# A fused attention block on one core: transposes of the first step in another order over more banks, and the decay of the queries behind the joins in every step

## What is computed

```python
xn = layernorm(x)                                   # 4 x 512 x 512
q, k, v = split(silu(xn @ w_qkv.T))                 # 16 heads of 128
for each chunk of each head:                        # kernel: chunks of 128 tokens
    o  = (q * q_decay) @ kv                         # what earlier chunks left
    o += ((q @ k.T) * diag_decay) @ v               # inside the chunk
    kv = block_decay * kv + (k * k_decay).T @ v
o = norm_w * o * rsqrt(mean(o * o) + eps)
s = (sigmoid(xn @ w_gate.T) * o) @ w_out.T
g = silu(xn * sum(topk(softmax(xn @ router.T))) + topk weights @ expert_bias)
out = x + s * g
```

## Time and profile before

| | us |
|---|---|
| median of three executions | 1141.87 (1141.83 to 1143.33) |
| the profiled execution | 1140.82 |
| its span in the trace | 1139.0 |
| busy: PE, DVE, ACT, POOL | 1095.3, 626.9, 509.2, 564.0 |

### The profile page before, as it was taken

How to read it: one execution, slowest core, us unless ns; L and a number is a source line. 1 busy time by engine, 2 the same in 40 slices (tenths; PEclk the granted TensorE clock), 3 DMA queues, 4 the chain that set the end, 5 groups by cost and what they waited for, 6 DMA issues and landing times.

```text
span 1139.0 us, 17081 instructions
## 1 busy us (share of the span) xinstructions
PE 1095.3 (96%) x6546; PEld 965.4 (85%) x6546; DVE 626.9 (55%) x1080; ACT 509.2 (45%) x813; POOL 564.0 (50%) x450
## 2 busy tenths in 40 slices
PE   6988999999999999999999899999999999999995
PEld 5877889898888989888897788989888898989874
DVE  6644464545646454557648646454554636365666
ACT  6645253353525335462544525334353534446242
POOL 4456354464536445273637736445453644536244
PEclk9998999999999999999999999999999999999998
DMA  7353110111111011112813111011111111011021
GB/s 247 109 184 96 56 38 20 56 38 38 41 52 38 24 53 38 37 41 90 313 39 130 57 55 38 21 55 37 38 56 38 38 38 47 28 38 42 15 75 74
DMA packets 28079, 73.10 MB, mean 64 GB/s; under 512 B 3040, under 2 KB 3168, under 8 KB 28000
## 3 DMA queue, kind: packets, MB, share of 16 engines
q1 hardware_dynamic: 28000, 72.02, 19.3%
HBM read 59.43 MB, written 12.58 MB: 63 GB/s over the span
## 4 chain that ended last, share of the span: by engine, by line
PE 87%; DVE 8%; POOL 2%; ACT 1%; issue 1%; DMA 1%; POOLq 0%; SPq 0%; DVEq 0%; ACTq 0%
PE st_ps L459 12%; PE st_ps L461 12%; PE st_ps L460 12%; PE v_ps L547 5%; PE v_ps L549 5%; PE v_ps L548 5%; PE out_ps L609 5%; PE head_ps L599 5%; PE out_ps L610 5%; PE out_ps L611 5%; PE head_ps L602 4%; PE tk_ps L584 4%; PE score_ps L573 3%; DVE q_t L1554 3%; DVE gate_lo L1579 1%
## 5 line engine op out<-in xcount | busy, mean ns | idle before, releaser
L459 PE MATMUL st_ps<-xt_hi,w_hi 128*128 128x512 f32 x630 | 259.5, 412 | 9.6 <-DVE gated L1530 5.7
L461 PE MATMUL st_ps<-xt_hi,w_lo 128*128 128x512 f32 x630 | 248.0, 394 | 0.0
L460 PE MATMUL st_ps<-xt_lo,w_hi 128*128 128x512 f32 x630 | 246.5, 391 | 0.0
L1279 POOL TENSOR_TENSOR w_lo<-land_a,w_hi 128x768 fp32r<-128x768 f32 x45 | 82.8, 1840 | 235.1 <-ACT w_hi L910 235.1
L1588 DVE TENSOR_TENSOR acc<-acc,out_ps 128x512 f32<-128x512 f32 x120 | 82.4, 687 | 211.3 <-PE out_ps L611 211.2
L1297 POOL TENSOR_TENSOR w_lo<-land_a,w_hi 128x1024 fp32r<-128x1024 f32 x45 | 111.7, 2483 | 112.1 <-ACT w_hi L915 112.1
L459 PEld LDWEIGHTS st_ps<-xt_hi,w_hi 128*128 128x128 f32 x630 | 119.2, 189 | 32.5 <-DVE gated L1530 8.0
L461 PEld LDWEIGHTS st_ps<-xt_hi,w_lo 128*128 128x128 f32 x630 | 118.7, 188 | 26.6
L460 PEld LDWEIGHTS st_ps<-xt_lo,w_hi 128*128 128x128 f32 x630 | 119.4, 190 | 20.8
L547 PE MATMUL v_ps<-wv_hi,xt_hi 128*128 128x256 f32 (+1 forms) x472 | 135.8, 288 | 0.0
L549 PE MATMUL v_ps<-wv_hi,xt_lo 128*128 128x256 f32 (+1 forms) x472 | 134.4, 285 | 0.0
(11 more groups left out here) (289 smaller groups left out, 2222.2 us busy)
## 6 DMA issues: line engine op xcount, KB each, us to landing
land_a<-wgrp_dram SPq DMA_DIRECT2D x48, 512.0 KB, 3.7
land_b<-wv_dram SPq DMA_DIRECT2D x16, 512.0 KB, 3.7
land_b<-wo_dram SPq DMA_DIRECT2D x16, 512.0 KB, 3.6
xt_hi<-spill_hi SPq DMA_DIRECT2D x16, 256.0 KB, 5.1
xt_lo<-spill_lo SPq DMA_DIRECT2D x16, 256.0 KB, 5.7
out_dram<-acc SPq DMA_DIRECT2D x16, 256.0 KB, 2.0
spill_hi<-gate_hi SPq DMA_DIRECT2D x11, 256.0 KB, 2.1
spill_lo<-gate_lo SPq DMA_DIRECT2D x11, 256.0 KB, 2.5
```

Of the source, the lines that this page charges most:

```text
L459: pe.matmul(ps[:, :], w_h2, x_h2, start=first and k == 0, stop=False, skip_group_check=True)
L460: pe.matmul(ps[:, :], w_h2, x_l2, start=False, stop=False, skip_group_check=True)
L461: end = pe.matmul(ps[:, :], w_l2, x_h2, start=False, stop=last and k == 1, skip_group_check=True)
L1279: pool.tensor_tensor(flat(w_lo[:, buf, 0:3, :, :]), flat(land_a[:, 0:3, :, :]), flat(w_hi[:, buf, 0:3, :, :]).bitcast(F32), ALU.subtract). ...
```

## The change

In every step on DVE, `decay_scores` is split in `score_decay` (the scores) and `query_decay` (the queries). In the last group of a step both `query_decay` and `gate_low(ss,0,0)` move behind `e4`, `e5` and the second `score_decay`. In step 8 the row work `sum0(7)`, `scale0(6)`, `scale0(7)` and `scale0(0)` moves as well.

In step 0 the fills of half 0 come two by two and earlier, in two banks; `direct_block` uses two banks instead of three, and `st_ps[2]` becomes a bank for fills of half 1; a new function says which fill last used a bank. On POOL three token sums go ahead of the low parts of the third weight group. The wait for the spills with `gate_high(0,0,0)` and `out_hi(0,0)` on ACT, `gate_low(0,0,0)` on DVE and `out_lo(0)` on POOL move from the end of step 0 into step 1.

```diff
+        fill_order = [(0, f) for f in range(11)]
+        fill_order += [(0, 11), (1, 0), (0, 12), (0, 13), (1, 1), (0, 14), (0, 15)] + [(1, f) for f in range(2, 16)]
...
         def fill_bank(bp, f):
             if bp == 0:
-                return (out_ps, tk_ps, score_ps, head_ps)[f % 4] if f < 8 else out_ps
-            return head_ps if f < 8 else (v_ps, out_ps)[f % 2]
+                return (out_ps, tk_ps, score_ps, head_ps)[f % 4] if f < 8 else (out_ps, head_ps)[f % 2]
+            free = [st_ps[2]] * 3 + [out_ps, head_ps, st_ps[2], out_ps, head_ps, st_ps[2], out_ps, v_ps]
+            return (free + [st_ps[2], out_ps, v_ps, st_ps[2], out_ps])[f]
...
-                n, buf, ps = j // 4, j // 4 % 2, st_ps[j % 3]
-                if j >= 3:
-                    pe.wait_ge(acted, j - 2)
+                n, buf, ps = j // 4, j // 4 % 2, st_ps[j % 2]
+                if j >= 2:
+                    pe.wait_ge(acted, j - 1)
...
                 act_c11(ss, QK0)
+                if ss == 1:
+
+                    for i in range(3):
+                        act.wait_ge(spilled[i], 32 * (16 // 3 + (i == 0)))
+                    gate_high(0, 0, 0)
                 take_square(before, 1, 0)
...
                 act_c12(ss, QK0)
+                if ss == 1:
+                    out_hi(0, 0)
...
+            for i in range(3):
+                token_sum1(i)
             direct_lo(2, 0)
             direct_lo(2, 1)
-            token_sum1(0)
-            token_sum1(1)
-            token_sum1(2)
+            token_sum1(3)
...
                 e3(ss, GATE)
-                gate_low(ss, 0, 0)
...
-                decay_scores(ss, 1, 0)
-                if close:
-                    sum0(7)
-                    scale0(6)
+                score_decay(ss, 1, 0)
...
                 e4(ss, GATE)
                 e5(ss, GATE)
-                decay_scores(ss, 1, 1)
+                score_decay(ss, 1, 1)
+                if close:
+                    sum0(7)
+                    scale0(6)
...
-                if close:
-                    scale0(7)
+                query_decay(ss, 1, 0)
+                gate_low(ss, 0, 0)
+                query_decay(ss, 1, 1)
                 states(ss, odd, 1, 0)
...
                 e7(ss, GATE)
                 gate_head(ss, 0, 1)
+                if close:
+                    scale0(7)
```

More of the change, by code:

```diff
@@ L220, in fill_bank, with fill_bank_left @@
             if bp == 0:
-                return (out_ps, tk_ps, score_ps, head_ps)[f % 4] if f < 8 else out_ps
-            return head_ps if f < 8 else (v_ps, out_ps)[f % 2]
+                return (out_ps, tk_ps, score_ps, head_ps)[f % 4] if f < 8 else (out_ps, head_ps)[f % 2]
+            free = [st_ps[2]] * 3 + [out_ps, head_ps, st_ps[2], out_ps, head_ps, st_ps[2], out_ps, v_ps]
+            return (free + [st_ps[2], out_ps, v_ps, st_ps[2], out_ps])[f]
+        def fill_bank_left(bp, f):
+            at = fill_order.index((bp, f))
+            before = [i for i in fill_order[:at] if fill_bank(*i) is fill_bank(bp, f)]
+            return before[-1] if before else None
         def direct(j):
@@ L407, in fill @@
                 b, k = rows_of(f)
-                if bp == 0 and f >= 4:
-                    pe.wait_ge(xt_l, filled(0, f - 4 if f <= 8 else f - 1))
-                if bp == 1 and f == 8:
+                left = fill_bank_left(bp, f)
+                if left is not None:
+                    pe.wait_ge(xt_l, filled(*left))
+                if fill_bank(bp, f) is v_ps:
                     pe.wait_ge(v_taken, 4)
-                elif bp == 1:
-                    pe.wait_ge(xt_l, filled(0, 7) if f == 0 else filled(1, f - 1) if f < 8 else
-                               filled(0, 15) if f == 9 else filled(1, f - 2))
                 if f // 2 in (T1, T3, T2, T4):
@@ L480, in p2 @@
                     pe.wait_ge(v_taken, v_before(ss) + TILES)
+                if group(ss, g) == 3:
+                    pe.wait_ge(acted, 12)
                 block_product(st_ps[1], buf, A12, B21, True, True)
@@ L779, in _ @@
             fill(0, 8)
+            fill(0, 9)
             direct_block(4)
-            fill(0, 9)
+            fill(0, 10)
+            fill(0, 11)
             fill(1, 0)
@@ L784, in _ @@
             direct_block(5)
-            fill(0, 10)
+            fill(0, 12)
+            fill(0, 13)
             fill(1, 1)
             v_fill(0, 0, 2)
-            fill(0, 11)
+            fill(0, 14)
+            fill(0, 15)
             fill(1, 2)
@@ L900, in act_direct @@
                     act.wait_ge(xt_turned, filled(1, 3))
-                act.activation(direct(j)[2], st_ps[j % 3][:, :], func, scale=scale).then_inc(acted, 1)
+                act.activation(direct(j)[2], st_ps[j % 2][:, :], func, scale=scale).then_inc(acted, 1)
             def raw_hi(n, buf):
@@ L1161, in _ @@
             take_fill(0, 8)
-            direct_hi(2, 0)
-            direct_hi(2, 1)
+            take_fill(0, 9)
+            for c in range(NCH):
+                normalise(2, 1, 1, c)
+            act_direct(4)
+            take_fill(0, 10)
+            take_fill(0, 11)
+            take_fill(1, 0)
+            take_k_rows(0, 0, 0, 0)
+            act_direct(5)
+            take_fill(0, 12)
+            take_fill(0, 13)
             act.wait_ge(ffn_const_in, 48)
@@ L1166, in _ @@
             act.activation(expert_hi[:, :], expert_row[:, :], ACT.Copy).then_inc(ffn_const_h, 1)
[L1167 to L1172, removed]
             take_fill(1, 1)
-            for c in range(NCH):
-                normalise(2, 1, 1, c)
+            direct_hi(2, 0)
+            direct_hi(2, 1)
             take_v(0, 0, 2)
-            take_fill(0, 11)
+            take_fill(0, 14)
+            take_fill(0, 15)
             take_fill(1, 2)
@@ L1414, in _ @@
             weight_sums(3)
-            token_sum1(3)
             sums_lo(3, 1)
@@ L1695, in step @@
                 e5(ss, QK0)
+                if ss == 1:
+                    gate_low(0, 0, 0)
                 gate_low(before, 1, 0)
@@ L1698, in step @@
                 e7(ss, QK0)
-                decay_scores(ss, 0, 0)
-                decay_scores(ss, 0, 1)
+                score_decay(ss, 0, 0)
+                query_decay(ss, 0, 0)
+                score_decay(ss, 0, 1)
+                query_decay(ss, 0, 1)
                 router(3)
@@ L1719, in step @@
                     sum0(1)
+                states(ss, odd, 0, 0)
+                if close:
                     scale0(0)
-                states(ss, odd, 0, 0)
                 if last:
@@ L1811, in _ @@
                 normalise(1, 0, c)
-            take_fill(0, 8)
+            for f in range(8, 12):
+                take_fill(0, f)
+            take_fill(1, 0)
+            score_decay(0, 0, 0)
+            query_decay(0, 0, 0)
+            take_fill(0, 12)
+            take_fill(0, 13)
+            take_fill(1, 1)
             dve.wait_ge(ffn_const_h, 1)
```

100 lines of the change are left out of this document (42 added, 58 removed).

## The result

The changed kernel takes **1179.7 us** (median of four executions, 1178.49 to 1181.1), against 1142.36 of the kernel before run beside it (1141.83 to 1143.33): ratio 1.0326, 95% interval 1.0308 to 1.0344. It is slower by 3.3%. The forecast was 1182, the range 1169 to 1197. The profiled execution has a span of 1179.3 us, where before had 1139.0.

A forecast was written before the change was run, and what follows sets the result against it. PE's own work bounds the steady steps, so only PE's waits count. Terms -5.4 + 40.3 + 2 - 5 + 0 + 8 = +40 gave a median of 1182 us, range 1169 to 1197.

The forecast's parts named there:

- e4: Join of the GATE group on DVE (L1530); PE waited for it 12 times, 5.7 us; forecast to start earlier, waits gone.
- part 1: Join `e4` starts earlier on DVE, so PE's 11 waits of 0.49 us vanish: -5.4 us.
- part 2: Boundaries between steps: longer DVE chain, and the second query decay waits for POOL; 13 x 3.1 = +40.3 us.
- steps 8 and 9: Step 8 and the boundary into 9: the 3.36 us wait goes, about 5.4 comes: +2, between 0 and +5.
- step 0: Fill waits of 6.3 us go, a 1.2 us wait of the third direct block comes: -5.1, taken as -5.
- step 1: First `p6`: the 3.7 us wait goes, 3.3 to 4.9 at `head_output` replaces it: 0, between -1 and +2.
- clock falls: Clock falling behind the new boundary waits: +8 us; none costs 0, a fall behind each 13 x 1.6 = 21.
- the first rival: At boundaries, second decay issued before POOL asks, or DVE keeps the port: 0.83 us each, 1141 to 1144; chance 0.10.
- The two costs inside it: At each boundary, `p6` waits 0.83 us from the longer DVE chain alone, 3.1 with the second decay behind POOL.
- the edits at nothing: Changes priced at 0: POOL's token sums, new waits of query decays, `p2` and `p5`, `scale0(0)` and `scale0(7)`.
- what is late next: Step 1, after the spill wait: ACT's `raw_hi` needs a late load, so PE waits 3.3 to 4.9 us for the square.
- The case without falls: At boundaries POOL blocks the second decay, but the clock stays up: 1174 us, chance 0.25.

The follow-up runs named there:

- the two fastest kernels: Changed kernel with both operations in DVE's gap, step 1's load before spill 13, `scale0(7)` back: 1121.99 us; same plus `out_hi(0,0)` between the activations: 1122.42 us.

## Why the prediction was right

The sign, the place and the size held. Point by point, against the profiled execution (1139.0 to 1179.3 span, +40.3):

| term | predicted | measured |
|---|---|---|
| part 1, `e4` | -5.4, in 11 steps | -4.7, in the nine ordinary ones (0.5 each, 2 to 5, 7, 10 to 13) |
| part 2, 13 boundaries | +40.3 (3.1 each) | +41.6 (3.2 each) |
| steps 8 and 9, without the boundary into 8 and the clock | +2 | +1.9 (the `e4` of step 9 included) |
| step 0, to the begin of step 1 | -5 | -4.2 (-5.6 in the run with only step 0 changed) |
| step 1 | 0 | +1.2 (its `e4` included) |
| clock falls | +8 | +4.3 |
| sum | +40 | +40.1, and 0.2 not placed |

**Part 1** held as told: the wait was due to the stretched decay ahead of it, and nothing took its place there in the nine ordinary steps. In step 9 the gain doesn't show: in the two fastest kernels that step is as long as before (66.3), with a new wait of 0.7 for the first join.

**Part 2** held in its times as well. If the predicted times are moved by the 1.61 us by which the changed kernel is later at this place, they read against the trace: first decay 227.36 (227.36), `gate_low` 227.83 (227.83), POOL asks 228.08 (228.08), end of the second decay 231.3 (231.18), `p6` 234.98 (234.86). The choice that carried it, that POOL gets in between two DVE operations that follow each other, was read from two operations at the very end of the program. It holds at all 13 boundaries: each time the second decay takes 2.75 or 2.76 us and POOL's `wo_lo` 2.69. The Trainium skill (SBUF — State Buffer, Who interferes with whom) says that issue order, not the shape of an operation, decides who blocks. The runs agree: with `gate_low` in between POOL is first and the decay takes 2.75, without it the decay is first and takes its half of 1.02, and POOL takes 2.58 in place of 2.41. That the first rival turned on 0.35 us was right too: 0.6 us less ahead of the decay changes the side.

The two costs inside it held as well. Measured in step 4 against the kernel with both operations in DVE's gap, `p6` starts 3.05 us later in the changed kernel (forecast 3.1), 0.86 with POOL late (forecast 0.83 without a block) and 0.25 with one decay in the chain (forecast 0.47 less 0.24). In all three another 0.15 is lost some 6 us further on, at `head_output`, which the prediction did not have; its cause is not isolated. This is how 3.05 becomes the 3.2 of a step.

**Steps 8 and 9** together went from 141.8 to 148.4 us, +6.6; without 3.2 for the boundary into 8 and 1.5 for the clock +1.9 is left. The sum was right by luck, since its place was half wrong. The prediction had 5.4 us come through `sum0(7)` and `k_row`. The wait for `k_row` in step 8 is 2.8; the other 2.6 are two waits for the square in step 9, through `scale0(7)`, POOL's `finish0(7)` and `add_square`. The prediction had put `scale0(7)` among the edits at nothing, as 0.7 us beside PE's work. It looked at what the operation costs on DVE and not at who waits for its result.

**Step 0**: the fill term is right (-5.6 measured where nothing else differs), and so is the wait of 3.6 us for the square that replaces the 3.7. The step that failed is "what is late next": it stopped at the square, and gave no price to `out_hi(0,0)`, which the change also moves into step 1. Behind the square ACT comes late to `k_row` as well, 1.2 us that PE feels. The remaining 1.4 us between 83.6 and 85.0 are TensorE's clock in the first block products, told below.

**Clock**: this is the term that was mis-sized most. The clock fell at 165.9, 650.6 and 729.1. Only the first and the last are behind boundaries, two and not the five that 8 us stands for at 1.6 each; they made steps 2 and 10 longer by 1.5 and 1.3 us (69.9 and 69.7 against 68.4). The one in step 8 stands behind the wait for `k_row`, where the prediction had no fall; it has nothing to compare it to, and is put at 1.5 as an estimate from the other two. Together that is 4.3. The bounds 0 and 21 held; nothing in the trace of before could say which boundaries it would be, and the runs here do not say it either. The case without falls (1174) and the forecast (1182) can't be told apart by this term of 4 us; the measured time lies between them.

## What to carry over

Where two engines share a path and the first to ask gets it, the room to look at is the distance between the moment at which the one asks and the moment at which the other's operation is issued. Placing an operation with two SBUF inputs directly behind another opens a slot for the waiting engine, and what follows pays the length of the other's operation, here 2.2 us for the 0.6 of `gate_low`. When work has to leave a critical place, look for a stretch in which its engine waits: the same two operations cost 3.2 us a step behind DVE's wait for a buffer and nothing ahead of it. And an operation that is "beside other work" on its own engine is free only if nobody waits for its result.

## What was not expected of the hardware

In some executions the first block products of the program ran at half speed for a few us longer. The same stretch in the changed kernel and in the kernel before:

```profile
13.70:18.60 4.90, 3.40 (x9) 2.75 (x9) 4.47 (x13) 2.23 (x4) 2.39 (x2) 1.00 1.05 359
```

```profile
13.70:18.60 4.90, 3.40 (x16) 2.84 (x16) 4.47 (x13) 2.22 (x4) 2.43 (x2) 1.00 1.05 351
```

Both show 3.40 us of busy PE, in one 9 matmuls and in the other 16. (The clock column says 1.00 in both, but the trace records no clock before 18.8 us in the one and 13.7 in the other, and the first matmuls took 0.76 us in the one and 0.47 in the other.) The new code is not enough to bring it: the run with only step 0 changed has the 16, and the kernel with the load moved and the one with `scale0(7)` back, with the same instructions up to there, begin step 1 at 85.0 and 83.8. PE's first long wait, ahead of its first products, is 9.7 to 10.1 us in all of these kernels. So 1 to 1.4 us at the begin come and go between profiled executions of the new step 0, five of eight with the late clock. The two of the old step 0 both have the early one, too few to say whether the change has a part in it.
